# Two graph layers, an expert layer and a dense layer in float32 on one core: a new order and another split of the work in the first layer

## The chip, the cores and the metric

The kernel runs on one core of a Trainium2 chip. The metric is the time of one execution on the device in microseconds (us). TensorE (PE in the profile) multiplies, VectorE (DVE), ScalarE (ACT) and GpSimd (POOL) work on elements, and SyncE (SP) issues most of the DMAs.

## What is computed

The adjacency matrix M is 4096 x 4096, the input x is 4096 x 128, all in float32. Each of two blocks is a graph layer and an expert (FFN) layer. The change touches only the first graph layer of the first block, called the first layer here:

```
A = M / (sum of M over rows + 1e-8)
W = A where A > 1e-6, else 0
T = h @ W_in + b_in
agg = (W^T @ T) / (sum of W over rows + 1e-8)    (T itself for a column without an entry)
out = agg @ W_out + b_out + h @ W_self + b_self
h = relu(layernorm(out) * gamma + beta)
```

h is the layer norm of x. D_in is 128, the hidden width of this layer is 256. A second layer of the same form (256 to 128) follows with the same M, then a gate and eight experts, then in the second block M times the hidden state and a routed FFN.

## The kernel before

M is cut into eight blocks of 512 columns (`NB = 8`, `BW = 512`). A block is 4096 x 512 float32, 8.4 MB, and is loaded in four quarters of 2 MB into one of two slots of `ring` (two slots of 128 KB a partition in all). The first layer goes over the blocks from the last to the first, block k of this order in slot k % 2. Of each block three engines make use while it is in its slot:

- DVE adds its 32 row tiles into two halves of R (`add_quarter`, L826: 15 adds of 128 x 1024 a block) and folds these (`fold`, L834) into pA, 128 partial sums a column. PE sums pA over the partitions with a matrix of ones (`sums`, L1310), and by columns (L1312), into SR and SM.
- ACT checks with an activation that counts (`check`, L533) whether any entry lies in the range in which the threshold could matter. DVE reduces the counts to `bad` (`verdict`), PE sums it (`sum_verdict`, L1323), and DVE reads the flag (L872) and masks the block only if it is set (`mask_if_needed`). With these inputs it is not.
- PE multiplies the block by S, the normalised input (`products`, L1330: 32 products of 128 x 512 a block, each in two records in the trace).

PE forms these column sums twice a block: `raw_sums(k)` (for the threshold) and again at the start of the step (`sums(BT, s_ms)`, the sums after a possible mask). DVE writes the threshold of each block (L853), the indicator of empty columns (L893, 128 x 512), and in `scales` a chain of small operations on 128 x 4 (L894 to L913).

What follows for a block, one step later: DVE adds product and indicator to aT (`collect` and L967). PE multiplies aT and hT (the transposed input, staged by POOL, turned by `turn_h`, copied by ACT at L546) by the joint weights, 256 wide (`out_rows`, L1345 and L1346), tiles 0 and 1 and then 2 and 3. POOL makes the bias rows (L691, L693). DVE adds all three into z1 (`out_tiles`), takes the moments (L785, L788), waits for the inverse root from POOL (L669) and normalises (L937). PE turns z1 (`turn_z`, L1358), ACT applies gamma, beta and relu (L552), PE multiplies by the weights of the second layer (`layer2_products`, L1369), and DVE adds biases into U and R (`layer2_inputs`). POOL adds the node's own T for empty columns (`own_T2`).

Nothing is scheduled by a planner. Each engine has its queue written out by hand in its `step`, and semaphores tie them. On PE the pieces stand between the products: out_rows 0, 1 after product 12 of the step, raw_sums after 18, out_rows 2, 3 after 21, turn_z after 30, sum_verdict after 31, and after the last product layer2_products and turn_h. The first product of a step waits for `s_clean`, which DVE sets once the flag is read and the block masked or not. DVE's order in a step is scales, layer2_inputs, aT, quarter 3 and fold of the next block, out_tiles 0, 1, quarter 0 of the block after it, thresholds, out_tiles 2, 3, normalise, verdict, the flag, quarters 1 and 2. SP issues quarter q of block k+2 once PE is through quarter q of block k, and the last one after the block (`refill`).

Of the kernel before, what the change touches and what calls it, by code (L numbers as in the profile page):

```python
# [69 lines left out]
SUM_MAX = 4.0 / 4096.0 / THRESH  # L70
FMAX = 3.4028234e38
# [6 lines left out]
def build(nc, A, out):  # L78
    ctx = ExitStack()
    with ctx:  # L80
# [37 lines left out]
        sumc, rs_, ws_, rw_, nn = [small[:, 4 * i:4 * i + 4] for i in range(5)]  # L118
        rbp, cc = [[small[:, 72 + 8 * i + 4 * j:76 + 8 * i + 4 * j] for i in range(2)] for j in range(2)]
# [13 lines left out]
        pA, thr, aT, hT, hs = [part(BW * i, BW) for i in range(5)]  # L133
        pre = [part(5 * BW + DH * i, DH) for i in range(2)]
# [93 lines left out]
        zeros = R[:, t_at + 1920:t_at + 1920 + BW]  # L228
# [27 lines left out]
        s_ms = sem("s_ms")  # L256
# [3 lines left out]
        s_thr = sem("s_thr")  # L260
# [9 lines left out]
        s_hs = sem("s_hs")  # L270
# [3 lines left out]
        s_o1u = sem("s_o1u")  # L274
        s_pre = sem("s_pre")
# [82 lines left out]
        def peeled1(eng, step):  # L358


            for k in range(NB):
                step(k, k % 2, k // 2, {d: 0 <= k + d < NB for d in (-2, -1, 1, 2)})

        def scan(eng, k):


            return (NB - 1) - k

# [16 lines left out]
        def _(sp):  # L385
            load_quarter(sp, adjc, scan(sp, 0), 0, 0)
# [3 lines left out]
            for q in range(1, 4):  # L390
                load_quarter(sp, adjc, scan(sp, 0), 0, q)
            for dst, name in WEIGHTS:
                sp.dma_start(dst, A[name]).then_inc(s_wts, 16)
            for q in range(2):
                load_quarter(sp, adjc, scan(sp, 1), 1, q)

            sp.wait_ge(s_thrst, 16)
            for q in range(2, 4):
                load_quarter(sp, adjc, scan(sp, 1), 1, q)

            def store_thr(k):
                sp.wait_ge(s_thr, k + 1)
                alone(sp)
                sp.dma_start(thr_d[ds(scan(sp, k), 1), :], thr[0:1, :]).then_inc(s_thrst, 16)

            def refill(k, slot):
                for q in range(3):

                    sp.wait_ge(s_quart, (k - 2) * 3 + q + 1)
                    alone(sp)  # L410
                    load_quarter(sp, adjc, scan(sp, k), slot, q)
                store_thr(k - 1)
                sp.wait_ge(s_agg, k - 1)
                alone(sp)
                load_quarter(sp, adjc, scan(sp, k), slot, 3)

            refill(2, 0)
# [5 lines left out]
            for q in range(4):  # L423
                n = E1 * CAP // 4
                sp.dma_start(disp_d[q * n:(q + 1) * n, :].rearrange("(p t) r -> p (t r)", p=P), fill).then_inc(s_fill, 16)
            for k in range(3, NB):
                refill(k, k % 2)
# [15 lines left out]
            def tail_inputs():  # L443

                sp.wait_ge(s_u2u, 2 + 2 * NB)
# [76 lines left out]
        def _(act):  # L522
            def check(k, slot, rnd, q):

                if q == 0 and k > 0:
                    act.wait_ge(s_bad, k)
                    alone(act)
                act.wait_ge(s_ring[slot][q], (rnd + 1) * 16)
# [8 lines left out]
            for q in range(4):  # L537
                check(0, 0, 0, q)

            act.wait_ge(s_thr, 1)  # L540
            act.dma_start(thr_d[NB - 1:NB, :], thr[0:1, :]).then_inc(s_thrst, 16)
            act.wait_ge(s_wts, 16 * len(WEIGHTS))

            def evac_hT(k):
                act.wait_ge(s_hTp, k + 2)
                nc.scalar.copy(hT, T[0][:, :]).then_inc(s_hT, 1)  # L546

            def relu_h1(k):

                act.wait_ge(s_zT, k)  # L550
# [5 lines left out]
            def step(k, slot, rnd, has):  # L556
                if has[1]:
                    check(k + 1, 1 - slot, rnd + slot, 2)
                    check(k + 1, 1 - slot, rnd + slot, 3)
                if has[2]:  # L560
                    check(k + 2, slot, rnd + 1, 0)
                    check(k + 2, slot, rnd + 1, 1)
                if has[-1]:
                    relu_h1(k)
                evac_hT(k)

            check(1, 1, 0, 0)
            check(1, 1, 0, 1)
            peeled1(act, step)
            relu_h1(NB)  # L570


# [74 lines left out]
        def _(pool):  # L647
# [31 lines left out]
            def stage(k):  # L679

                pool.wait_ge(s_hTp, k + 1)
                alone(pool)
                nc.gpsimd.tensor_copy(hs, S[:, ds(scan(pool, k) * BW, BW)]).then_inc(s_hs, 1)

            def bias_rows(kk, slot):
                pool.wait_ge(s_msp, kk + 1)
                alone(pool)
                for t in range(BT):
                    pool.wait_ge(s_o1u, kk * BT + t + 1)
                    alone(pool)  # L690
                    nc.gpsimd.tensor_scalar(pre[t % 2], b_io[:, :], cc[slot][:, t:t + 1], None, ALU.mult)  # L691
                    pool.drain()
                    nc.gpsimd.tensor_tensor(pre[t % 2], pre[t % 2], b_all[:, :], ALU.add).then_inc(s_pre, 1)  # L693

            def own_T2(kk):

                blk = scan(pool, kk)
                pool.wait_ge(s_u2u, kk * 2 + 4)
                alone(pool)
                cols = ds(blk * BW, BW)  # L700
# [960 lines left out]
```

## Time and profile before

| | before |
|---|---|
| median of 3 runs | 1170.33 us (1165.82 to 1171.22) |
| the profiled execution | 1171.33 us |
| its span, first to last instruction | 1169.6 us |
| mean granted TensorE clock | 0.965 |
| PE busy | 1049.7 us (90%) |
| DVE busy | 586.1 us (50%) |
| ACT busy | 299.3 us (26%) |
| POOL busy | 303.7 us (26%) |

The profile shows one execution, and its times below count from the first instruction; 1.7 us of the execution lie outside the span. The shares are over the whole kernel; the first layer is roughly its first 390 us, in which DVE is much busier than later. The chain of waits gives DVE's adds (L826) 12% of the whole span, all of it in the first layer. A PE time includes a modelled end of some 0.17 us that overlaps the next instruction.

### The profile page before, as it was taken

How to read it: one execution, taken by the hardware profiler on the slowest of the kernel's cores; microseconds unless marked ns; L12 is line 12 of the kernel's file. 1: busy time of each engine (PE TensorE's matmuls, PEld its weight loads, DVE VectorE, ACT ScalarE, POOL GpSimd, SP SyncE). 2: the span in 40 equal slices, each digit the busy share in tenths (PEclk: the TensorE clock that was granted, in tenths of full speed). 3: DMA queues.
4: the chain of work that ended last, by engine and by line, in shares of the span. 5: the costliest groups of instructions: out<-in, count | busy, mean ns of one | idle time of the engine just before them, and what ended most of it. 6: DMA issues, size and time to landing. Idle time of an engine off the chain costs nothing.

```text
span 1169.6 us, 13701 instructions
## 1 busy us (share of the span) xinstructions
PE 1049.7 (90%) x4004; PEld 610.9 (52%) x4004; DVE 586.1 (50%) x1560; ACT 299.3 (26%) x594; POOL 303.7 (26%) x303
## 2 busy tenths in 40 slices
PE   0598989989999999999996599679999999999996
PEld 0344545545555554444442388424766756667655
DVE  6867778778763323434444168752243332422333
ACT  4542624434400000000000045232212222212222
POOL 4703254354243412222222135541011010110110
PEclk9889999999999999999998699879999999999998
DMA  9859555455400278888671643147354454453200
GB/s 359 331 187 350 208 216 198 166 212 206 154 1 1 80 284 304 312 317 312 266 301 69 248 144 118 50 144 287 145 224 164 181 188 182 179 225 145 82 10 10
DMA packets 44894, 221.00 MB, mean 189 GB/s; under 512 B 6610, under 2 KB 27412, under 8 KB 33170
## 3 DMA queue, kind: packets, MB, share of 16 engines
q1 hardware_dynamic: 41872, 215.47, 49.4%
q0 software_dynamic: 2944, 4.66, 1.2%
q8 instruction: 31, 0.51, 0.2%
q14 instruction: 45, 0.37, 0.1%
q10 hardware_dynamic: 2, 0.00, 0.0%
HBM read 210.68 MB, written 11.62 MB: 190 GB/s over the span
## 4 chain that ended last, share of the span: by engine, by line
PE 67%; DVE 19%; issue 4%; ACT 2%; DVEq 2%; POOL 2%; DMA 1%; SPq 1%; ACTq 0%; POOLq 0%
PE PA L1330 26%; PE PA L1516 19%; DVE R L826 12%; PE O L1555 5%; PE O L1492 3%; PE SR L1555 2%; PE SM L1555 2%; ACT U L595 2%; PE T L1563 1%; PE O L1538 1%; PE PA L1482 1%; PE O L1369 1%; POOL small L669 1%; PE T L1358 1%; PE SR L1421 1%
## 5 line engine op out<-in xcount | busy, mean ns | idle before, releaser
L1516 PE MATMUL PA<-ring,S 128*128 128x512 f32 x512 | 234.5, 603 | 3.7 <-ACT S L613 2.9
L1330 PE MATMUL PA<-ring,S 128*128 128x512 f32 x512 | 232.8, 605 | 0.0
L1330 PE MATMUL PA<-ring,U 128*128 128x512 f32 x512 | 225.6, 595 | 0.0
L826 DVE TENSOR_TENSOR R<-R,ring 128x1024 f32<-128x1024 f32 x112 | 157.3, 1404 | 15.9 <-issue 9.4
L1255 DVE TENSOR_TENSOR U<-ring,work 128x512 f32<-128x512 f32 x128 | 93.7, 733 | 123.8 <-PE SR L1555 49.9
L1330 PEld LDWEIGHTS PA<-ring,S 128*128 128x128 f32 x512 | 96.9, 194 | 105.3 <-issue 104.3
L1330 PEld LDWEIGHTS PA<-ring,U 128*128 128x128 f32 x512 | 95.1, 190 | 106.7 <-issue 106.5
L1516 PEld LDWEIGHTS PA<-ring,S 128*128 128x128 f32 x512 | 94.7, 193 | 106.0 <-issue 100.7
L533 ACT ACTIVATE work<-ring 128x2048 int8<-128x2048 f32 x64 | 122.3, 1910 | 107.0 <-DMA ring<-in_adj_cols 91.6
L774 POOL DMA_DIRECT2D out_x<-work x8 | 6.7, 842 | 285.5 <-DVE work L1281 285.5
L744 POOL DMA_INDIRECT disp_d<-work x32 | 32.2, 1008 | 122.7 <-DVE work L1128 115.4
L1555 PEld LDWEIGHTS O<-work,U 128*128 128x128 f32 x512 | 59.5, 192 | 6.9 <-issue 6.7
L1555 PE MATMUL O<-work,U 128*128 128x64 f32 x512 | 58.9, 274 | 0.0
L756 POOL DMA_INDIRECT y_d<-R,work x40 | 40.9, 1023 | 57.3 <-DVE R L1188 49.7
L638 ACT ACTIVATE U<-O,work 128x64 f32<-128x64 f32 x128 | 33.2, 310 | 71.2 <-PE O L1555 59.4
L1281 DVE TENSOR_TENSOR work<-T,work 128x512 f32<-128x512 f32 x8 | 5.5, 692 | 90.7 <-PE T L1563 90.7
L691 POOL TENSOR_SCALAR work<-b_io,small 128x256 f32<-128x256 f32 x32 | 43.1, 1347 | 21.8 <-DVE work L927 19.2
L666 POOL TENSOR_SCALAR small<-mv 128x4 f32<-128x4 f32 x32 | 7.7, 240 | 149.4 <-DVE mv L788 138.7
L718 POOL TENSOR_TENSOR U<-U,work 128x512 f32<-128x512 f32 x8 | 14.0, 1753 | 109.5 <-ACT work L546 109.5
L581 ACT COPY work<-T 128x512 f32<-128x512 f32 x8 | 4.7, 585 | 137.4 <-PE T L1415 137.4
L552 ACT ACTIVATE work<-T,gb 128x512 f32<-128x512 f32 x16 | 11.6, 773 | 109.2 <-PE T L1358 109.2
L1492 PE MATMUL O<-work,U 128*128 128x128 f32 x320 | 37.9, 278 | 1.0 <-ACT U L595 0.6
(212 smaller groups left out, 1242.1 us busy)
## 6 DMA issues: line engine op xcount, KB each, us to landing
ring<-in_adj_cols SPq DMA_DIRECT2D x56, 2048.0 KB, 7.3
ring<-in_adjT_cols SPq DMA_DIRECT2D x32, 2048.0 KB, 7.2
ring<-in_Wr SPq DMA_DIRECT2D x1, 4096.0 KB, 12.3
ring<-in_Wr SPq DMA_DIRECT2D x2, 2048.0 KB, 13.3
work<-in_w SPq DMA_DIRECT2D x16, 256.0 KB
disp_d<-U SPq DMA_DIRECT2D x4, 650.0 KB, 13.1
work<-disp_d SPq DMA_DIRECT2D x8, 325.0 KB, 3.2
S<-in_x SPq DMA_DIRECT2D x4, 512.0 KB, 8.9
```

The costliest lines, as they stand in the source:

```text
L533: last = nc.scalar.activation(junk, src, ACT.Gelu, scale=GELU_SCALE, accum_out=csum[slot][:, col:col + 1])
L595: nc.scalar.activation(e_hm[:, f * CAP + c * CAP // 2:f * CAP + (c + 1) * CAP // 2], HB[q % 4][:, 0:CAP // 2], ACT.Relu, bias=e_b1[par][:, ...
L638: last = nc.scalar.activation(dst[:, m * BW + s * SEG:m * BW + (s + 1) * SEG], LB[n // SH][:, at:at + SEG], ACT.Relu, bias=b_r[:, ds(e + ( ...
L691: nc.gpsimd.tensor_scalar(pre[t % 2], b_io[:, :], cc[slot][:, t:t + 1], None, ALU.mult)
L744: nc.gpsimd.indirect_dma_start(disp_d, bass.IndirectOffsetOnAxis(ap=idx[:, t:t + 1], axis=0), rows[:, t * ROW:(t + 1) * ROW], None, bounds ...
L756: nc.gpsimd.indirect_dma_start(y_d, bass.IndirectOffsetOnAxis(ap=e_idx[par][:, q:q + 1], axis=0), e_y[par][:, q * D:(q + 1) * D], None, bo ...
L826: nc.vector.tensor_tensor(acc, first if q == 0 and c == 1 else acc, piece, ALU.add)
L1255: nc.vector.tensor_tensor(wst[n % WS], ring[0][l][:, ds(e * (KH * DH), KH * DH)], w_s[:, l * KH * DH:(l + 1) * KH * DH], ALU.add).then_inc ...
L1330: mm = nc.tensor.matmul(out_T[:, :], X[:, t * D:(t + 1) * D], ring[slot][t // HT][:, (t % HT) * BW:(t % HT + 1) * BW], start=n == 0, stop= ...
L1492: mm = nc.tensor.matmul(bank[:, c * D:(c + 1) * D], e_hm[:, f * CAP + q * P:f * CAP + (q + 1) * P], e_w2[par][:, f * D:(f + 1) * D], start ...
L1516: mm = nc.tensor.matmul(PA[slot][:, :], S[:, t * D:(t + 1) * D], ring[1][t // HT][:, (t % HT) * BW:(t % HT + 1) * BW], start=t == 0, stop= ...
L1555: mm = nc.tensor.matmul(LB[g][:, at:at + SEG], wst[n % WS][:, kk * DH + m * P:kk * DH + (m + 1) * P], src[:, kk * BW + s * SEG:kk * BW + ( ...
```

## The change

- The sums are formed once a block on PE (`raw_sums`). Threshold and masked sums are made by DVE only in the branch that masks (`masked_sums`), and the per-node sums are copied to SBUF (`ms`).
- The indicator of empty columns is made by ACT (`empty_cols`, L542) from SR. ACT also writes cc times the bias row into z1 (`bias_rows`, L553), and normalises (L561) with a scale and a bias that POOL makes (`moments`). POOL adds the constant bias in one 128 x 1024 operation (`add_bias`). It stages nothing for `turn_h` any more; PE turns from S. hT is double.
- The order in a step is new on every engine. Block 1's last two quarters no longer wait for a threshold store. The zeros for clearing y_d lie in U rather than R.

The diff, cut to what the orders and these operations are:

```diff
@@ SP
-            for q in range(2):
-                load_quarter(sp, adjc, scan(sp, 1), 1, q)
-            sp.wait_ge(s_thrst, 16)
-            for q in range(2, 4):
-                load_quarter(sp, adjc, scan(sp, 1), 1, q)
+            for q in range(4):
+                load_quarter(sp, adjc, blk(1), 1, q)
...
@@ ACT
+            def empty_cols(k):
...
+                act.wait_ge(s_sums, k + 1)
+                alone(act)
+                nc.scalar.activation(U[:, cols_of(k)], SR[:, :], ACT.Relu, bias=ones[:, 0:1], scale=EMPTY_SCALE).then_inc(s_ind, 1)
...
+            def bias_rows(k):
+                act.wait_ge(s_msp, k + 1)
+                alone(act)
+                for t in range(BT):
+                    last = nc.scalar.activation(z1[:, t * DH:(t + 1) * DH], b_io[:, :], ACT.Copy, scale=cc[k % 2][:, t:t + 1])
+                last.then_inc(s_pre0, 1)
+            def normalise(k):
+                act.wait_ge(s_rstd, k + 1)
+                alone(act)
+                for t in range(BT):
+                    zt = z1[:, t * DH:(t + 1) * DH]
+                    last = nc.scalar.activation(zt, zt, ACT.Identity, bias=nm[:, t:t + 1], scale=rstd[:, t:t + 1])
+                last.then_inc(s_z, 1)
...
+            for k in range(NB):
+                evac_hT(k)
+                if k + 1 < NB:
+                    check(k + 1, 3)
+                if k > 0:
+                    normalise(k - 1)
+                    relu_h1(k - 1)
+                bias_rows(k)
+                if k + 1 < NB:
+                    empty_cols(k + 1)
+                if k + 2 < NB:
+                    for q in range(3):
+                        check(k + 2, q)
...
@@ POOL
+            for k in range(NB):
+                empty_rows(k)
+                if k > 0:
+                    moments(k - 1)
+                add_bias(k)
+                if k > 0:
+                    own_T2(k - 1)
...
@@ DVE
-            def thresholds(k):
...
-                nc.vector.tensor_scalar(thr, SR[:, :], EPS, THRESH, ALU.add, ALU.mult)
...
+            def verdict(k):
+                dve.wait_ge(s_sums, k + 1)
+                alone(dve)
+                nc.vector.tensor_copy(ms, SM[:, 0:BT])
+                nc.vector.tensor_scalar(sumc, SM[:, 0:BT], EPS, None, ALU.add)
+                dve.wait_ge(s_cnt, k + 1)
...
             def scales(k):
-                nc.vector.tensor_scalar(U[:, ds(blk * BW, BW)], SR[:, :], 0.0, None, ALU.is_le)
...
-                dve.wait_ge(s_rstd, k)
-                alone(dve)
-                for t in range(BT):
-                    zt = z1[:, t * DH:(t + 1) * DH]
-                    last = nc.vector.tensor_scalar(zt, zt, mv8[:, t, 0:1], rstd[:, t:t + 1], ALU.subtract, ALU.mult)
...
+            def step(k):
+                if k > 0:
+                    collect(k - 1)
+                if k + 1 < NB:
+                    add_quarter(k + 1, 2)
+                if k > 0:
+                    out_tiles(k - 1)
+                if k + 1 < NB:
+                    add_quarter(k + 1, 3)
+                    fold(k + 1)
+                if k + 2 < NB:
+                    add_quarter(k + 2, 0)
+                if k + 1 < NB:
+                    verdict(k + 1)
+                if k > 0:
                     layer2_inputs(k - 1)
+                if k + 1 < NB:
+                    mask_if_needed(k + 1)
+                    scales(k + 1)
+                if k + 2 < NB:
+                    add_quarter(k + 2, 1)
...
@@ PE
-            def step(k, slot, rnd, has):
                 pe.wait_ge(s_clean, k + 1)
-                sums(BT, s_ms)
-                pe.wait_ge(s_aT, k + 1)
...
+            L1_PIECES = ((2, lambda k: turn_h(k)),
+                         (4, lambda k: k > 0 and out_rows(k - 1, (0, 1))),
+                         (10, lambda k: k > 0 and out_rows(k - 1, (2, 3))),
+                         (18, lambda k: k > 0 and turn_z(k - 1)),
+                         (21, lambda k: k + 1 < NB and raw_sums(k + 1)),
+                         (25, lambda k: k > 0 and layer2_products(k - 1)),
+                         (29, lambda k: k + 1 < NB and sum_verdict(k + 1)))
...
```

How the queues moved, at three places. First PE from the product that sums the verdict (SM) to the next out_rows (O from W_io and W_s), before:

```order
L1323 MATMUL SM<-ones,small 1x1
L1330 MATMUL PA<-ring,S 128x512
L1369 MATMUL O<-W_us,work 128x256 x8
L1351 MATMUL T<-ident,work 128x128 x4
L1310 MATMUL SR<-work,ones 128x512
L1312 MATMUL SM<-ones,work 128x1 x4
L1330 MATMUL PA<-ring,S 128x512 x12
L1345 MATMUL O<-W_io,work 128x256
L1346 MATMUL O<-W_s,work 128x256
```

and now:

```order
L1341 MATMUL SM<-ones,small 1x1
L1348 MATMUL PA<-ring,S 128x512 x5
L1372 MATMUL T<-ident,S 128x128 x4
L1348 MATMUL PA<-ring,S 128x512 x2
L1364 MATMUL O<-W_io,work 128x256
L1365 MATMUL O<-W_s,work 128x256
```

The second sums and layer2_products are gone from this stretch, and 7 products stand in it in place of 13.

Second, DVE around aT (work from PA and U) of the last block, before (the small operations are the end of scales):

```order
L909 TENSOR_TENSOR small<-small 128x4
L911 TENSOR_TENSOR small<-small 128x4
L913 TENSOR_TENSOR small<-small 128x4
L949 TENSOR_TENSOR U<-O,b_us 128x256
L950 TENSOR_TENSOR R<-O,b_us 128x256
L949 TENSOR_TENSOR U<-O,b_us 128x256
L950 TENSOR_TENSOR R<-O,b_us 128x256
L967 TENSOR_TENSOR work<-PA,U 128x512
L826 TENSOR_TENSOR R<-R,ring 128x1024 x4
```

and now:

```order
L951 TENSOR_TENSOR small<-rb,small 128x4
L952 TENSOR_TENSOR small<-small,ne 128x4
L954 TENSOR_TENSOR small<-small,ne 128x4
L848 TENSOR_TENSOR R<-R,ring 128x1024 x4
L989 TENSOR_TENSOR work<-PA,U 128x512
L848 TENSOR_TENSOR R<-R,ring 128x1024 x4
L965 TENSOR_TENSOR work<-O,work 128x256
L967 SCALAR_TENSOR_TENSOR work<-O,small,work 128x256
```

Between scales and aT now stand four adds; layer2_inputs left this place.

Third, DVE from the verdict to the reading of the flag, before:

```order
L788 BN_AGGR mv<-st 128x2 x4
L937 TENSOR_SCALAR work<-work,mv,small 128x256 x4
L862 TENSOR_REDUCE small<-small 128x1
L864 TENSOR_SCALAR small<-small 128x1
L866 SCALAR_TENSOR_TENSOR small<-small 128x1
L872 CAST flags<-SM 1x1
```

and now:

```order
L879 TENSOR_REDUCE small<-small 128x1
L880 TENSOR_SCALAR small<-small 128x1
L882 SCALAR_TENSOR_TENSOR small<-small 128x1
L979 TENSOR_TENSOR U<-O,b_us 128x256
L980 TENSOR_TENSOR R<-O,b_us 128x256
L979 TENSOR_TENSOR U<-O,b_us 128x256
L980 TENSOR_TENSOR R<-O,b_us 128x256
L919 CAST flags<-SM 1x1
```

Between verdict and flag DVE now waits for layer2_products and adds its results.

## Rows read from the trace of the kernel before

**Rows 1.** Busy time by engine in one step (start:end, length, busy us and instructions)
```profile
219.00:263.00 44.00, 40.51 (x134) 22.00 (x134) 34.83 (x62) 18.36 (x21) 18.92 (x14) 1.00 0.50 192
```
**Rows 2.** Timeline of DVE, one step: start, us, instructions, idle before
```profile
226.39 6.17 DVE L826 TENSOR_TENSOR R<-R,ring 128x1024 f32<-128x1024 f32 x4 [0.19 <-issue]
232.75 0.69 DVE L893 TENSOR_SCALAR U<-SR 128x512 f32<-128x512 f32 x1 [0.19 <-issue]
...
235.38 0.16 DVE L913 TENSOR_TENSOR small<-small 128x4 f32<-128x4 f32 x1
...
237.08 0.68 DVE L967 TENSOR_TENSOR work<-PA,U 128x512 f32<-128x512 f32 x1
237.68 7.08 DVE L826 TENSOR_TENSOR R<-R,ring 128x1024 f32<-128x1024 f32 x4
244.94 0.70 DVE L834 TENSOR_TENSOR work<-R 128x512 f32<-128x512 f32 x1 [0.18 <-issue]
245.95 0.42 DVE L925 TENSOR_TENSOR work<-O,work 128x256 f32<-128x256 f32 x1 [0.31 <-issue]
...
255.69 1.41 DVE L785 BATCH_NORM_STATS2 st<-work 128x6 f32<-128x256 f32 x4
257.17 0.38 DVE L788 BATCH_NORM_AGGREGATE mv<-st 128x2 f32<-128x6 f32 x4
259.36 1.38 DVE L937 TENSOR_SCALAR work<-work,mv,small 128x256 f32<-128x256 f32 x4 [1.82 <-POOL small L669]
...
263.08 0.15 DVE L872 CAST flags<-SM 1x1 int32<-1x1 f32 x1 [1.80 <-PE SM L1323]
264.35 5.13 DVE L826 TENSOR_TENSOR R<-R,ring 128x1024 f32<-128x1024 f32 x4 [1.12 <-issue]
```
**Rows 3.** Timeline of PE: pieces of one step, and 18 products of layer two
```profile
220.13 3.62 PE L1369 MATMUL O<-W_us,work 128*128 128x256 f32 x16
...
224.02 1.02 PE L1310 MATMUL SR<-work,ones 128*128 128x512 f32 x2
224.88 0.95 PE L1312 MATMUL SM<-ones,work 128*128 128x1 f32 x8
...
237.86 0.67 PE L1345 MATMUL O<-W_io,work 128*128 128x256 f32 x2 [1.62 <-DVE work L967]
...
260.89 1.06 PE L1358 MATMUL T<-ident,work 128*128 128x128 f32 x8 [1.15 <-DVE work L937]
...
427.93 15.62 PE L1330 MATMUL PA<-ring,U 128*128 128x512 f32 x36
```
**Rows 4.** Groups by line on ACT: busy us, mean ns | idle before
```profile
L552 ACT ACTIVATE work<-T,gb 128x512 f32<-128x512 f32 x16 | 11.6, 773 | 109.2 <-PE T L1358 109.2
L610 ACT ACTIVATE S<-R,work 128x128 f32<-128x128 f32 x24 | 7.4, 387 | 34.2 <-POOL work L669 34.2
```
**Rows 5.** Timeline of POOL beside DVE's adds of 226.39
```profile
224.99 2.34 POOL L718 TENSOR_TENSOR U<-U,work 128x512 f32<-128x512 f32 x1 [9.47 <-ACT work L546]
```
**Rows 6.** Stretches after two stalls of PE; PEclk is third from last
```profile
74.00:80.70 6.70, 6.70 (x15) 3.66 (x14) 4.31 (x9) 4.01 (x4) 0.00 (x0) 0.51 0.19 78
...
108.10:111.40 3.30, 3.30 (x9) 2.65 (x10) 3.15 (x3) 0.00 (x0) 0.00 (x0) 0.52 1.09 367
```
**Rows 7.** Timeline of PE, the first two blocks
```profile
49.51 2.07 PE L1310 MATMUL SR<-work,ones 128*128 128x512 f32 x2 [2.19 <-POOL S L676]
...
73.10 1.52 PE L1310 MATMUL SR<-work,ones 128*128 128x512 f32 x2 [2.64 <-DVE work L834]
...
107.87 1.19 PE L1345 MATMUL O<-W_io,work 128*128 128x256 f32 x2 [4.52 <-issue]
```
**Rows 8.** Timeline of DVE: the last copy before block 0's verdict
```profile
45.05 0.28 DVE L1007 COPY b_us<-O 128x128 f32<-128x128 f32 x1
```
**Rows 9.** Timeline of PE: out_rows of blocks 5 and 7
```profile
324.49 0.67 PE L1345 MATMUL O<-W_io,work 128*128 128x256 f32 x2 [1.19 <-DVE work L967]
...
393.96 0.60 PE L1345 MATMUL O<-W_io,work 128*128 128x256 f32 x2
```

More of the change, by code:

```diff
@@ L118, in build @@
         sumc, rs_, ws_, rw_, nn = [small[:, 4 * i:4 * i + 4] for i in range(5)]
+        ms, nm = [small[:, 64 + 4 * i:68 + 4 * i] for i in range(2)]
         rbp, cc = [[small[:, 72 + 8 * i + 4 * j:76 + 8 * i + 4 * j] for i in range(2)] for j in range(2)]
@@ L130, in part @@
             return work[:, at:at + n]
-        pA, thr, aT, hT, hs = [part(BW * i, BW) for i in range(5)]
-        pre = [part(5 * BW + DH * i, DH) for i in range(2)]
+        pA, thr, aT = [part(BW * i, BW) for i in range(3)]
+        hT = [part(BW * i, BW) for i in (3, 4)]
+        own = part(5 * BW, BW)
         z1 = part(6 * BW, BT * DH)
@@ L953, in collect @@
             def collect(k):
[L955 removed]
+                dve.wait_ge(s_agg, k + 1)
                 alone(dve)
[L957 removed]
+                dve.wait_ge(s_neh, k + 1)
                 alone(dve)
[L960 to L987 removed]
@@ L991, in _ @@
+            add_quarter(0, 0)
+            add_quarter(0, 1)
             dve.wait_ge(s_rstd0, 1)
@@ L1007, in _ @@
             nc.vector.tensor_copy(b_us[:, 0:D], O[1][:, 2 * D:3 * D]).then_inc(s_wready, 1)
-            thresholds(0)
-            verdict(0, 0)
-            mask_if_needed(0, 0)
-            for q in range(3):
-                add_quarter(1, 0, q)
-            peeled1(dve, step)
-            layer2_inputs(NB - 1)
-            collect(NB)
-            nc.vector.tensor_tensor(aT, PA[1][:, :], U[:, 0:BW], ALU.add).then_inc(s_aT, 1)
-            out_tiles(NB, 1, range(BT))
-            normalise(NB)
-            layer2_inputs(NB)
+            verdict(0)
+            mask_if_needed(0)
+            scales(0)
+            for q in range(2):
+                add_quarter(1, q)
+            for k in range(NB):
+                step(k)
+            collect(NB - 1)
+            out_tiles(NB - 1)
+            layer2_inputs(NB - 1)
             dve.wait_ge(s_own, NB)
@@ L1371, in layer2_products, with step @@
                         mm.then_inc(s_u2, 1)
-            def step(k, slot, rnd, has):
-                pe.wait_ge(s_clean, k + 1)
-                sums(BT, s_ms)
-                pe.wait_ge(s_aT, k + 1)
-                products(S, slot, 0, 12, s_quart)
-                if has[-1]:
-                    out_rows(k, (0, 1))
-                products(S, slot, 12, 18, s_quart)
-                if has[1]:
-                    raw_sums(k + 1)
-                products(S, slot, 18, 21, s_quart)
-                if has[-1]:
-                    out_rows(k, (2, 3))
-                products(S, slot, 21, 30, s_quart)
-                if has[-1]:
-                    pe.wait_ge(s_hT, k)
-                    turn_z(k)
-                products(S, slot, 30, 31, s_quart)
-                if has[1]:
-                    sum_verdict(k + 1)
-                products(S, slot, 31, NT, s_quart).then_inc(s_agg, 1)
-                if has[-1]:
-                    layer2_products(k)
-                turn_h(k)
-            raw_sums(0, True)
+            L1_PIECES = ((2, lambda k: turn_h(k)),
[5 more added lines that the diff above has]
+                         (29, lambda k: k + 1 < NB and sum_verdict(k + 1)))
+            def step(k):
+                pe.wait_ge(s_clean, k + 1)
+                if k >= 2:
+                    pe.wait_ge(s_aT, k - 1)
+                done = 0
+                for n, piece in L1_PIECES:
+                    products(S, k % 2, done, n, s_quart)
+                    piece(k)
+                    done = n
+                products(S, k % 2, done, NT, s_quart).then_inc(s_agg, 1)
+            raw_sums(0)
             sum_verdict(0)
             pe.wait_ge(s_hn, 2)
-            peeled1(pe, step)
+            for k in range(NB):
+                step(k)
             def tail_a(k):
```

355 lines of the change are left out of this document (165 added, 190 removed).

## The prediction

> **What bounds the kernel now.** I read the page first: the change touches only the first layer, so only its 390 us count. Next I took busy times by stage. In one step of the first layer PE is busy 40.5 us of 44 and DVE 34.8 [rows 1]. PE looks like the bound, but the timelines say otherwise. PE waits for DVE at three places of each step: 1.62 us before out_rows, until aT is there; 1.15 us before turn_z, until z is normalised [rows 3]; and 0.7 us before raw_sums. DVE waits only 1.82 us for POOL's inverse root, 1.80 us for the flag and 1.12 us in the branch behind it [rows 2]. So **DVE's queue is the chain**: its work, small gaps and three short waits fill the step. From out_rows of block 0 at 107.87 to that of block 5 at 324.49 are five steps [rows 7, 9]: 216.6 us, or **43.3 a step**.
>
> I call the start of the first out_rows in a step s. The question is what s to s will be, when the first s comes, and how long it is from the last full step to out_rows of block 7, which starts layer two at 393.96 [rows 9].
>
> **What goes and what comes, per step.**
> - PE: the second sums go, 1.65 us (1.02 and 0.95 without their modelled ends) [rows 3].
> - DVE: L893 goes to ACT, 0.61 without the end that the next operation overlaps; the threshold, of the same form, 0.61; the normalise 1.3, with its wait of 1.82; a copy, a compare and one drained step of scales, some 0.25. The copy `ms` adds 0.1. About 2.8 us of work and 1.8 of waiting [rows 2].
> - POOL: the staging copy and eight bias operations go, one of 128 x 1024 and two tiny ones come. POOL slows DVE: four adds take 5.13 us when it rests, 6.17 with 2.5 us of it beside them, 7.08 under a long run [rows 2, 5]. Aside from the place named below, I cost its new work at nothing: it lies where DVE has slack.
> - ACT: the indicator 0.7, four bias rows and four normalises of 128 x 256. By 128 x 128 at 0.31 (7.4 us for 24) and 128 x 512 at about 0.7 a time [rows 4], four take 1.6 to 1.9. ACT is busy 18 of 44 us [rows 1] and has room. Only the normalise is on a path.
>
> If nothing else bound, PE's own work would: 32 products 27.5, out_rows 3.5, layer2_products 3.45, turn_z, turn_h, sums and flag 3.1 [rows 3], about 37.5 us a step. I don't believe this, because of the order.
>
> **The loop that remains.** With times from s:
> - PE from s to the flag: four tiles of out_rows 3.5, 25 products at 0.86 (15.62 for 18) 21.5, turn_z 0.87, sums 1.65, layer2_products 3.45, the flag 0.15 [rows 3]: 31.1.
> - Does turn_z wait? PE is there at s+15.55. DVE has two tiles of out_tiles done at s+7.1 (0.9 each), but tile 3 leaves PE only at s+8.7, so the moments end at s+11.6 [rows 2]. Inverse root 1.8, two more small POOL operations 0.5, normalise on ACT 1.75, semaphores: s+15.8. A wait of 0.3. The fold is done at s+18.1, PE wants it at s+19.1: no wait. Sum s+31.4.
> - DVE meanwhile is through with its adds and verdict at s+23.4 and then waits for layer2_products (s+26 and s+27.8) and again for the flag. Here its saved work ends as **idle time**.
> - Then DVE in series: semaphore 0.1, flag to next operation 1.27, scales 2.8 - 0.61 - 0.25 = 1.95, gap 0.2, quarter 1 of the next block but one, gap 0.25, aT 0.68, semaphore 0.1 [rows 2]. The four adds take 5.13 to 7.08; POOL multiplies the indicator by hT just then (2.34 us when contended [rows 5]), which is the case of 6.17. I take 6.1. Sum 10.6.
>
> So s to s is 31.4 + 10.6 = **42.0 us**, 41.0 with uncontended adds, 43.0 with the slowest. PE in the meantime has only 7 products and turn_h, 6.45 us, to do. It then stands still for about 4.15 us, at one place rather than three.
>
> **The clock.** Such a stall has a price in this trace. After 4.52 us of idling at 107.87 the granted clock was 0.52, the level of 1.2 GHz, for 3.3 us; after 2.64 us, followed by one-column products, 0.51 for 6.7 us [rows 6, 7]. The stalls of 1.6 us did nothing. A 3.4 us stretch at half clock costs 1.7. A stall of 4.15 lies between, nearer to the one of 4.52, but when it begins to count probably varies, and part of the slow stretch can fall into the stall itself. I take 1.0 a step between ends of 0 and 1.7. **Forecast per step: 43.0**, ends 41.0 and 44.7.
>
> The Trainium skill (TensorE: Matmul & The Clock Gate, HAM oscillation) says that a kernel whose matmuls pause too long in every iteration starts each one cold. By that rule the full 1.7 would come each step, 43.7, and the steady steps would lose a little; it speaks against this change, and the row at 107.87 agrees with it.
>
> **The start.** Block 0's second sums go, so products begin at 49.5 [rows 7], where POOL's normalised x arrives. DVE's last copy ends at 45.3 [rows 8]; verdict 0.95, flag 0.4, branch 1.3 to 1.5, scales 1.95: 50.2. Fifteen adds of block 1 at 1.3 with gaps 20.5, contention 1, fold 0.9: 72.5. PE needs 18.5 for 21 products and turn_h, plus 2 to 3 for the low clock it has there before too, and so waits briefly. Sums 1.65, eight products 6.9, so the flag goes at 81.1; flag, branch and scales 3.5, adds 6.1, gaps and aT 1.2: **first s at 92**, against 107.87. Why so much: PE does not wait through fold and sums of block 1, and out_rows moves from product 12 of a step to 4. The second part is handed back at the end.
>
> **The end.** The last full step starts five steps later: 92 + 215 = 307. In it there is no quarter 1 to add, so aT is there before PE wants it: 31.4 + 2.6 + 3.4 + 0.43 = 37.9 to the next s. From there 32.1 us of PE work without the sums and 3.4 of products to out_rows of block 7: 35.5. 307 + 37.9 + 35.5 = **380.4, against 393.96: 13.6 us less**. Behind it nothing moves: PE was dense there, z comes 1.1 later from ACT but the bias rows earlier, which is what DVE waited for.
>
> 1171.33 - 13.6 is 1157.7 for the profiled execution; the median of the runs shown is 1.0 below it, so **1157 us**.
>
> **The rivals.**
> 1. *The clock holds.* Same loop, but the stalls cost nothing: 42.0 a step, 5 us less than forecast: 1152. For: the stalls of 1.6 us are harmless. Against: 4.52 was not.
> 2. *Full overlap.* DVE's 12% in the chain of waits is really shed and PE's 37.5 to 38.5 us binds. 5 x 4.5 less than forecast: 1134. This needs DVE to pass flag, scales, adds and aT in the 6.5 us PE has for it; the rows give 10.6.
> 3. *The clock halves in every step, or ACT's share is longer.* 43.7 to 45.4 a step (slow stretches of 3.4 or 6.7 us): 1161 to 1169. At the upper end no change.
> 4. *Slower.* The mechanism: a slow stretch in each step makes PE late at sum_verdict and, if it begins again at the wait before turn_z, a second one follows. Two stretches of 6.7 us cost 6.7 a step: 48.7, 1157 + 28 = 1185. It decides from 46.6 a step, where the gain of start and end is used up and 6 us more. For: the row of 2.64 us with 6.7 us of low clock. Against: there one-column products followed; here wide ones do.
>
> The change does what it says, by the orders of the queues; the branch is not taken before nor after.
>
> **How the numbers follow.** Forecast 0.45, clock holds 0.20, full overlap 0.06, every step slow 0.21, slower 0.08. A measurement here can tell about 0.5%, 6 us, from no change. Faster by over 6 us: the first three, and half of the fourth, with a little off for a first s that comes late (a stall of 3 us before raw_sums would add a slow stretch): 0.76. Same 0.16, slower 0.08. The unknown costs (adds 41.0 to 43.0 a step, clock 0 to 1.7, first s 90 to 94, runs that differ by 5 us) make 1145 to 1168, which leaves out full overlap and slower.
>
> **What the profile after would show.** s at 92, and 42 to 43.7 us a step; PE's one long stall of about 4 us before out_rows, released by DVE's aT; DVE idle before layer2_inputs and the flag; PEclk under 1.00 in stretches behind some stalls; out_rows of block 7 at 380. I am wrong if the stall before out_rows is under 2 us, if turn_z waits over 1 us (ACT's normalise then sets the loop), or if layer two and later differ by more than 3 us.

## The result, and the profile after

The changed kernel takes **1190.2 us** (1188.9 to 1191.4, four runs) against 1170.35: a ratio of 1.0177 with an interval of 1.0148 to 1.0207. It is slower by 1.8%, where 1.1% faster was forecast, and lies outside the range. Times differ between chips: on one of those used below the kernel before took 1178.9 us. So kernels are compared by their ratio to the kernel before, run in the same group.

PE's timeline of one step after the change (start, us, what, idle before and its releaser), from one out_rows to the next:

```profile
239.41 1.19 PE L1364 MATMUL O<-W_io,work 128*128 128x256 f32 x2 [3.81 <-issue]
240.40 1.06 PE L1365 MATMUL O<-W_s,work 128*128 128x256 f32 x2
...
242.75 5.31 PE L1348 MATMUL PA<-ring,S 128*128 128x512 f32 x12
...
249.62 7.03 PE L1348 MATMUL PA<-ring,S 128*128 128x512 f32 x16
258.93 1.39 PE L1380 MATMUL T<-ident,work 128*128 128x128 f32 x8 [2.28 <-ACT work L561]
260.12 4.17 PE L1348 MATMUL PA<-ring,S 128*128 128x512 f32 x6
264.13 1.02 PE L1334 MATMUL SR<-work,ones 128*128 128x512 f32 x2
...
276.29 0.19 PE L1341 MATMUL SM<-ones,small 128*1 128x1 f32 x2
...
287.17 1.19 PE L1364 MATMUL O<-W_io,work 128*128 128x256 f32 x2 [4.05 <-issue]
```

A step is 47.8 us here, and 47.7 in the mean of five, from 96.23 to 334.91. Before it was 43.3 [rows 7, 9]. Each step has two stalls of PE, 3.8 to 4.05 us before out_rows, as forecast, and 2.3 to 2.7 before turn_z, which was not. Behind each the first instructions are slow: the first half of out_rows (four tile products) takes 3.3 us in place of 1.7, three products behind turn_z 4.0 in place of 2.6. Windows of time show why (start:end, length, busy us and counts, granted clock third from last):

```profile
239.50:242.60 3.10, 3.10 (x8) 2.47 (x9) 2.95 (x3) 2.27 (x3) 0.00 (x0) 0.51 0.00 0
242.70:256.60 13.90, 13.90 (x37) 6.67 (x36) 10.36 (x21) 1.64 (x2) 3.29 (x4) 1.00 0.48 170
259.70:262.90 3.20, 3.20 (x7) 1.64 (x7) 2.96 (x3) 2.54 (x6) 0.00 (x0) 0.50 0.55 236
```

PE runs at half clock, 1.2 GHz, behind both stalls, in every step; between them the clock is 1.00. The stretches after a stall in the kernel before read the same [rows 6].

DVE in the same step, from the moments to the flag and on to aT:

```profile
252.51 0.38 DVE L813 BATCH_NORM_AGGREGATE mv<-st 128x2 f32<-128x6 f32 x4
252.81 5.09 DVE L848 TENSOR_TENSOR R<-R,ring 128x1024 f32<-128x1024 f32 x4
...
266.08 0.16 DVE L873 COPY small<-SM 128x4 f32<-128x4 f32 x1 [3.27 <-PE SM L1336]
...
271.35 0.42 DVE L979 TENSOR_TENSOR U<-O,b_us 128x256 f32<-128x256 f32 x1 [4.38 <-PE O L1391]
...
276.63 0.15 DVE L919 CAST flags<-SM 1x1 int32<-1x1 f32 x1 [2.80 <-PE SM L1341]
278.16 0.18 DVE L938 RECIPROCAL small<-small 128x4 f32<-128x4 f32 x1 [1.39 <-issue]
...
280.05 6.03 DVE L848 TENSOR_TENSOR R<-R,ring 128x1024 f32<-128x1024 f32 x4
286.38 0.69 DVE L989 TENSOR_TENSOR work<-PA,U 128x512 f32<-128x512 f32 x1 [0.30 <-issue]
```

DVE idles for 3.27 us before the sums, 4.38 before layer2_inputs and 2.80 before the flag. The work taken from it, 2.8 us a step, became waiting. Its own chain from flag to aT lasts 10.5 us, in which PE has 7 products and turn_h.

Over the first layer: the first out_rows comes at 96.2 (before 107.9), that of block 7 at 414.5 (before 394.0 [rows 9]), so the layer is 20.5 us later at the point where layer two starts. The median is 19.9 longer; after that point the profiled execution wins back 2.7 us, which no run here explains.

### The profile page after: what moved, and what is told of

The parts are those of the page before. It is cut to its first block, busy times and chain, and to the rows that moved or that the text cites. A ratio compares the mean times of both kernels' runs of the same rounds, so it can differ in the third digit from the quotient of the medians.

```text
span 1187.4 us, 13419 instructions
## 1 busy us (share of the span) xinstructions
PE 1048.8 (88%) x3924; PEld 609.0 (51%) x3924; DVE 551.8 (46%) x1500; ACT 333.9 (28%) x666; POOL 245.6 (21%) x255
## 4 chain that ended last, share of the span: by engine, by line
PE 76%; DVE 8%; issue 4%; ACT 4%; POOL 2%; DMA 1%; DVEq 1%; SPq 1%; POOLq 1%; ACTq 0%
PE PA L1348 32%; PE PA L1532 18%; PE O L1571 5%; DVE R L848 3%; PE O L1508 3%; ACT U L620 2%; PE SR L1571 2%; PE SM L1571 2%; PE O L1391 2%; PE O L1364 2%; ACT work L561 1%; PE T L1579 1%; PE O L1365 1%; PE O L1554 1%; PE T L1380 1%
## 5 line engine op out<-in xcount | busy, mean ns | idle before, releaser
L1348 PE MATMUL PA<-ring,S 128*128 128x512 f32 x512 | 242.7, 623 | 3.0 <-POOL S L701 3.0
L1532 PE MATMUL PA<-ring,S 128*128 128x512 f32 x512 | 231.5, 596 | 4.7 <-ACT S L638 3.7
L1348 PEld LDWEIGHTS PA<-ring,S 128*128 128x128 f32 x512 | 100.8, 202 | 110.3 <-issue 105.6
L848 DVE TENSOR_TENSOR R<-R,ring 128x1024 f32<-128x1024 f32 x112 | 145.1, 1295 | 7.5 <-issue 0.9
L1532 PEld LDWEIGHTS PA<-ring,S 128*128 128x128 f32 x512 | 93.2, 190 | 105.3 <-issue 98.4
L1571 PEld LDWEIGHTS O<-work,U 128*128 128x128 f32 x512 | 59.4, 192 | 6.9 <-issue 6.7
L561 ACT ACTIVATE work<-work,small 128x256 f32<-128x256 f32 x32 | 16.6, 590 | 122.8 <-POOL small L729 122.8
L1364 PE MATMUL O<-W_io,work 128*128 128x256 f32 x64 | 25.4, 487 | 22.8 <-issue 22.8
L1508 PEld LDWEIGHTS O<-work,U 128*128 128x128 f32 x320 | 36.3, 192 | 3.2 <-ACT U L620 3.2
```

What stands on the lines that cost most here:

```text
L561: last = nc.scalar.activation(zt, zt, ACT.Identity, bias=nm[:, t:t + 1], scale=rstd[:, t:t + 1])
L848: nc.vector.tensor_tensor(acc, first if q == 0 and c == 1 else acc, piece, ALU.add)
L1348: mm = nc.tensor.matmul(out_T[:, :], X[:, t * D:(t + 1) * D], ring[slot][t // HT][:, (t % HT) * BW:(t % HT + 1) * BW], start=n == 0, stop= ...
L1364: nc.tensor.matmul(O[t % 2][:, 0:DH], aT[:, t * P:(t + 1) * P], W_io[:, :], start=True, stop=True)
L1508: mm = nc.tensor.matmul(bank[:, c * D:(c + 1) * D], e_hm[:, f * CAP + q * P:f * CAP + (q + 1) * P], e_w2[par][:, f * D:(f + 1) * D], start ...
L1532: mm = nc.tensor.matmul(PA[slot][:, :], S[:, t * D:(t + 1) * D], ring[1][t // HT][:, (t % HT) * BW:(t % HT + 1) * BW], start=t == 0, stop= ...
```

## The experiments

Theory A: the loop is the one of the prediction (PE from out_rows to the flag, then DVE from the flag to aT); its length exceeds 42.0 us because z is late, since POOL's small operations now run beside DVE's adds, and because the clock falls behind both stalls. The rivals: ACT's longer chain is the loop; POOL is slow for another reason; the clock falls for another cause; DVE's or the loads' own time binds.

Steps are means from the out_rows of block 0 to that of block 5. "Stalls" are PE's in a middle step, before out_rows / turn_z / raw_sums. PEclk is the granted clock from 100 to 380 us.

| kernel | ratio (95%) | step, us | stalls, us | PEclk |
|---|---|---|---|---|
| before | 1 | 43.3 | 1.6 / 1.15 / 0.7 | 0.99 |
| changed | 1.0177 (1.0148 to 1.0207) | 47.7 | 3.8 / 2.3 / 0 | 0.93 |
| e0, changed again | 1.0181 (1.0147 to 1.0214) | 47.5 | 3.8 / 2.3 / 0 | 0.93 |
| e1, turn_z later | 0.9979 (0.9954 to 1.0004) | 43.0 | 3.65 / 0 / 0 | 0.96 |
| e2, adds held | 1.0065 (1.0044 to 1.0085) | 45.5 | 4.0 / 0.5 / 0.4 | 0.96 |
| e3, warm | 1.0048 (1.0032 to 1.0065) | 44.8 | 0.4 / 2.3 / 0 | 0.99 |
| e5, e1 and e3 | 0.9886 (0.9854 to 0.9919) | 41.8 | 0.2 / 0 / 0 | 1.00 |
| e6, DVE's order | 1.0091 (1.0056 to 1.0125) | 46.4 | 0 / 2.3 / 3.6 | 0.94 |
| e7, PE's order | 0.9835 (0.9804 to 0.9865) | 41.3 | 2.0 / 0.6 / 0 | 1.00 |
| e4, both orders | 0.9690 (0.9668 to 0.9712) | 38.8 | 0 / 0.6 / 0 | 1.00 |
| e8, e4, normalise on DVE | 1.0011 (0.9997 to 1.0026) | 45.2 | 0 / 0 / 3.6 | 0.92 |
| e9, changed, sums twice | 0.9993 (0.9980 to 1.0007) | 44.5 | 1.0 / 2.3 / 0 | 0.98 |
| e11, e4, sums twice | 0.9772 (0.9756 to 0.9789) | 40.6 | 0 / 0.6 / 0 | 1.00 |
| e10, e4, one product later | 0.9618 (0.9602 to 0.9634) | 38.0 | 0 / 0 / 0 | 1.00 |

### The yardstick

The changed kernel, unedited.

> The changed kernel itself, unedited, as the yardstick of this group, since the kernel before took 1178.9 us on the chip of the last group rather than 1170.3. All theories: 1.015 to 1.02 of the kernel before, steps of 47.7 us.

1188.6 us, 1.0181, steps of 47.5: it repeats.

### turn_z behind raw_sums

```diff
-                         (18, lambda k: k > 0 and turn_z(k - 1)),
-                         (21, lambda k: k + 1 < NB and raw_sums(k + 1)),
+                         (21, lambda k: (k + 1 < NB and raw_sums(k + 1), k > 0 and turn_z(k - 1))),
```

> The changed kernel, but PE turns z behind raw_sums (both after product 21) rather than after product 18. In the changed kernel PE waits 2.3 to 2.7 us before turn_z in six steps, and the low clock behind that stall costs another 1.6 to 1.75. Theory A (the late z and the low clock behind it are what made a step 47.7 us rather than 42.0): both go, a step becomes 43.7 us, six steps give 24 us, so about 1166 us. Rival B (the loop hangs on ScalarE's chain of normalise, relu and bias rows, and the stall only moves to layer2_products or the flag): the step stays over 46.5 us and the time within 5 us of 1190.

Measured 1175.2 us beside 1178.9 of the kernel before, 0.9979. Against the ratio of the changed kernel this is 2.0% less, some 23 us. The stall before turn_z is gone and the steps are 41.9, 43.3, 41.9, 43.7 and 44.3 us: 43.0 in the mean. The two of 41.9 us are those without a slow stretch. One of them begins with a stall of 3.65 us before out_rows, behind which the clock stays at 1.00. The ten runs lie between 1170.3 and 1182.0 us, the longer ones at a lower mean clock (0.952 against 0.963 at the ends). Theory A holds, rival B falls.

### DVE's adds held back

```diff
                     out_tiles(k - 1)
+                    dve.wait_ge(s_rstd, k)
+                    alone(dve)
                 if k + 1 < NB:
                     add_quarter(k + 1, 3)
```

> The changed kernel, but DVE waits for the inverse root before it adds quarter 3, so nothing of DVE runs beside POOL's four small operations. In the changed kernel these take 3.7 us beside DVE's adds, in the kernel before the two of them took 1.5 with DVE idle. Theory A (contention makes z late): the four take 2.0 to 2.3 us, turn_z waits under 1 us, and no slow stretch follows: 44 to 45 us a step, about 1170 us; DVE's lost 2.3 us fall into its idle time. Rival C (the small operations of POOL are slow for another reason, such as more of them in a row): they stay near 3.7 us, the fold comes 4 us later, and the time is equal or worse, 1190 to 1210 us.

POOL's four operations in the changed kernel:

```profile
253.09 1.01 POOL L723 TENSOR_SCALAR small<-mv 128x4 f32<-128x4 f32 x1 [17.14 <-DVE mv L813]
254.18 1.18 POOL L724 TENSOR_SCALAR small<-mv 128x4 f32<-128x4 f32 x1
255.32 1.02 POOL L727 TENSOR_TENSOR small<-small,neg_half 128x4 f32<-128x4 f32 x1
256.48 0.20 POOL L729 TENSOR_TENSOR small<-small 128x4 f32<-128x4 f32 x1
```

and with the adds held back:

```profile
246.10 0.23 POOL L723 TENSOR_SCALAR small<-mv 128x4 f32<-128x4 f32 x1 [17.07 <-DVE mv L813]
246.41 0.19 POOL L724 TENSOR_SCALAR small<-mv 128x4 f32<-128x4 f32 x1
246.56 1.03 POOL L727 TENSOR_TENSOR small<-small,neg_half 128x4 f32<-128x4 f32 x1
247.73 0.20 POOL L729 TENSOR_TENSOR small<-small 128x4 f32<-128x4 f32 x1
```

From first start to last end they take 3.59 against 1.83 us, the way from the end of the moments to turn_z shrinks from 6.0 to 4.3 us, and the stall before turn_z falls from 2.3 to 0.5. So the first two operations, 0.2 us long by themselves, wait out a DVE add each, and rival C falls. The Trainium skill (SBUF — State Buffer, Who interferes with whom) has this: a DVE instruction with two SBUF inputs contends with a GpSimd instruction that reads SBUF, and whoever comes second waits until the other's instruction is over. This trace agrees: the delays of 0.8 and 1.0 us are under the 1.27 us of an add. The four adds run from 252.81 to 257.90, so by estimate one ends at 254.1 and the next at 255.4, and the two operations end at 254.10 and 255.36. The third and fourth operation are not lengthened; the third starts at 255.32, near the end of an add.

The step, 45.5, was a little above the 44 to 45 expected, and the gain 13 us rather than 20: raw_sums now waits 0.4 us, and two slow stretches behind out_rows last 6.8 us, not 3.4.

### Four products to fill the stall

```diff
-                         (4, lambda k: k > 0 and out_rows(k - 1, (0, 1))),
+                         (4, lambda k: k > 0 and (keep_warm(4 if k < NB - 1 else 0, S[:, 0:BW], T[1]), out_rows(k - 1, (0, 1)))),
```

> The changed kernel with four products of 128x512 into an unused bank of PSUM (their result is not read) ahead of out_rows 0 and 1 in the steps with a stall of 3.8 to 4.0 us there; they take 3.4 us at full clock. Theory A (the clock falls because PE stands still): PEclk stays 1.00 behind this stall, out_rows takes 1.7 us rather than 3.3, five or six steps give 1.6 us each, so 8 to 10 us less: about 1181 us. If the shorter step also keeps the second slow stretch, nothing more. Rival D (the clock at out_rows falls for another cause than the stall): the time stays 1190 us.

Ratio 1.0048, so some 15 us less than changed, more than the 8 to 10 expected. Four of the five steps are 44.3 to 44.5 us. The clock no longer falls at out_rows, and behind the stall of 2.3 us before turn_z, which is still there, it falls in one step of six only, the one in which this stall is 2.66 us and not 2.28. So the stall at out_rows causes its slow stretch (rival D falls). The second, for a stall of 2.3 us, depends on more than its length, since in the changed kernel it came each time.

### Both single edits

> The changed kernel with both single edits: PE turns z behind raw_sums, and four products of 128x512 whose result is not read fill the stall before out_rows. Theory A: with neither a late z nor any low clock the loop is what the walk in the prediction gave without a clock term, 42.0 us a step plus 0.5 because the four products start a moment late or end behind aT: 42.0 to 42.5, PEclk 1.00 from 100 to 400 us, and 28 to 32 us less than the changed kernel in the same group. Rival F (the low clock comes from the load on the chip and wanders whatever PE does): slow stretches remain and the steps stay at 43 to 44 us as with the first edit alone.

It combines the two diffs above.

```profile
100.00:380.00 280.00, 277.84 (x857) 149.03 (x856) 173.65 (x343) 126.30 (x166) 66.00 (x55) 1.00 0.43 167
```

PEclk is 1.00 throughout, steps are 41.9, 41.6, 41.8, 42.0 and 41.9 us, and the time is 1155.5 us, 33 less than e0, a little more than the 28 to 32 expected. This is the loop of the prediction, 42.0 without a clock term. Rival F falls. POOL's operations are as slow here as in the changed kernel; the 1.8 us that they lose fit in before turn_z at its new place.

### DVE's half of a better order

```diff
                 if k + 1 < NB:
-                    add_quarter(k + 1, 2)
+                    add_quarter(k + 1, 1)
                 if k > 0:
                     out_tiles(k - 1)
                 if k + 1 < NB:
+                    add_quarter(k + 1, 2)
                     add_quarter(k + 1, 3)
...
                     scales(k + 1)
-                if k + 2 < NB:
-                    add_quarter(k + 2, 1)
```

> Only DVE's half of the new order: aT straight behind scales, quarter 1 and out_tiles, then quarters 2 and 3. PE's queue as in the changed kernel. Theory A: aT comes early, but the fold now comes at s+23.4 while PE has raw_sums at s+19 to 21, so PE waits 2 to 4 us there, and z is 2.3 us late: 42 to 43 us a step without slow stretches, up to 45 with them; 15 to 30 us less than the changed kernel. Rival G (the adds between the flag and aT are the whole matter): 39 us a step or less.

Steps of 42.4 to 48.5 us, 46.4 in the mean, where at most 45 was expected; ratio 1.0091, 9 us less than e0 and not 15 to 30. The loop between flag and aT is gone; raw_sums takes its place, with PE coming too early for the fold:

```profile
246.51 1.09 PE L1378 MATMUL T<-ident,work 128*128 128x128 f32 x8 [2.29 <-ACT work L561]
247.44 2.74 PE L1346 MATMUL PA<-ring,S 128*128 128x512 f32 x6
253.79 2.07 PE L1332 MATMUL SR<-work,ones 128*128 128x512 f32 x2 [3.62 <-DVE work L856]
255.66 1.71 PE L1334 MATMUL SM<-ones,work 128*128 128x1 f32 x8
257.23 6.42 PE L1346 MATMUL PA<-ring,S 128*128 128x512 f32 x8
```

In this step the low clock lasts 10.2 us, from 252.4 on: the sums and four products take 9.7 us, and 5.3 in the step at full clock. In the other steps it lasts 3.4 or 6.8 us. Rival G falls: the adds alone are not the matter.

### PE's half

```diff
-                         (18, lambda k: k > 0 and turn_z(k - 1)),
-                         (21, lambda k: k + 1 < NB and raw_sums(k + 1)),
-                         (25, lambda k: k > 0 and layer2_products(k - 1)),
-                         (29, lambda k: k + 1 < NB and sum_verdict(k + 1)))
+                         (20, lambda k: k > 0 and turn_z(k - 1)),
+                         (23, lambda k: k > 0 and layer2_products(k - 1)),
+                         (24, lambda k: k + 1 < NB and raw_sums(k + 1)),
+                         (27, lambda k: k + 1 < NB and sum_verdict(k + 1)))
```

> Only PE's half of the new order: turn_z after product 20, layer2_products after 23, raw_sums after 24, the verdict's sum after 27. DVE's queue as in the changed kernel, so four adds still stand between flag and aT. Theory A: z is in time, the flag goes at about s+29.4, DVE's 10.7 us follow: 40 to 42 us a step, with a stall of 2.5 to 4 us before out_rows that sometimes costs a slow stretch; 30 to 40 us less than the changed kernel. Rival H (DVE's idle time is filled and its queue binds): 43 us or more.

Steps of 41.2 to 41.6 us, ratio 0.9835, some 40 us less than the changed kernel. The stall before out_rows is 2.0 to 2.4 us, less than the 2.5 to 4 expected, and the clock never falls behind it. DVE's idle time is used and its queue does not bind (rival H falls).

### Both halves

> The changed kernel in another order: DVE collects aT straight behind scales and adds quarter 1 after it, with quarter 2 behind out_tiles; PE has turn_z after product 20, layer2_products after 23, raw_sums after 24 and the verdict's sum after 27. Theory A (the adds between the flag and aT, and the place of turn_z, are all that keeps PE's work of 37.5 us a step from being the bound): no stall over 1 us, no slow stretch, 38 to 39 us a step, six steps give over 50 us: 1130 to 1140 us. Rival E (DVE's queue, then about 35 us a step with no idle left, or the later loads bind): 41 to 43 us a step, 1155 to 1165 us.

38.8 us a step, ratio 0.9690, which at 1170 us would be 1134. Rival E falls: with aT early and turn_z near its z, PE's work is the bound.

### All four pieces one product later

The places in e4 become 21, 24, 25 and 28.

> The reordered kernel with turn_z, layer2_products, raw_sums and the verdict's sum each one product later (21, 24, 25, 28). Theory A (PE is the bound, its one stall is the 0.57 us before turn_z): 38.1 us a step, ratio 0.965 to 0.968. Rival K (DVE comes next at once): 38.7 us or more, since flag, scales and aT move later by 0.86 us.

1125.9 us, **0.9618: by the ratios 45 us less than the kernel before, 65 less than the changed one**. A middle step of it on PE, without a stall, and DVE's aT 1.2 us before PE wants it:

```profile
199.40 1.88 PE L1346 MATMUL PA<-ring,S 128*128 128x512 f32 x4
201.12 0.59 PE L1362 MATMUL O<-W_io,work 128*128 128x256 f32 x2
...
219.16 1.04 PE L1378 MATMUL T<-ident,work 128*128 128x128 f32 x8
...
231.50 0.19 PE L1339 MATMUL SM<-ones,small 128*1 128x1 f32 x2
...
239.03 0.59 PE L1362 MATMUL O<-W_io,work 128*128 128x256 f32 x2
```

```profile
199.26 0.69 DVE L989 TENSOR_TENSOR work<-PA,U 128x512 f32<-128x512 f32 x1
```

Rival K falls. The gain was more than the 0.57 us a step: block 1's raw_sums no longer waits either (2.2 us in e4, with a slow stretch behind it), so out_rows of block 0 comes at 86.8 and not 90.1.

### The second sums, in the changed kernel and in e4

The sums of the kernel before, put back at the start of each step on data already there, with a result that is not read:

```diff
                 pe.wait_ge(s_clean, k + 1)
                 if k >= 2:
                     pe.wait_ge(s_aT, k - 1)
+                    pe.wait_ge(s_h1T, k - 1)
+                nc.tensor.matmul(T[1][:, :], ones[:, :], S[:, 0:BW], start=True, stop=True)
+                for t in range(BT):
+                    nc.tensor.matmul(T[1][:, t:t + 1], S[:, t * P:(t + 1) * P], ones[:, 0:1], start=True, stop=True)
```

> The changed kernel with a second group of column-sum products at the start of every step, as the kernel before has them (into an unused bank, on data already there, the result not read), 1.65 us of PE a step. Theory A (in the changed kernel's loop PE stands still there, so dropping the second sums bought nothing): the stall before out_rows shrinks by 1.65 us, the steps do not grow, and may shrink by 1.6 where the shorter stall no longer lowers the clock: ratio 1.005 to 1.018 of the kernel before. Rival J (PE's work counts): steps of 49.4 us, ratio 1.026 to 1.03.

Ratio 0.9993 against 1.0177: **1.65 us of needless work a step makes the changed kernel 1.8% faster**. The stall before out_rows is 1.0 to 1.4 us, the clock stays up there, and steps alternate between 43.4 (clock 1.00) and 45.3 us (one slow stretch behind turn_z):

```profile
226.53 0.67 PE L1364 MATMUL O<-W_io,work 128*128 128x256 f32 x2 [0.99 <-issue]
...
244.52 1.09 PE L1380 MATMUL T<-ident,work 128*128 128x128 f32 x8 [2.28 <-ACT work L561]
```

The ratio is below the band expected, 1.005 to 1.018. Of the gain 2 to 3.5 us come ahead of the steps: the first out_rows is at 92.7, against 96.2 in the changed kernel and 94.6 in e0. The rest fits the clock: three slow stretches from there on in place of twelve. Rival J falls.

> The reordered kernel with the same second group of sums at the start of each step. Theory A (PE is the bound there, so each us of PE counts): 40.3 us a step, eight steps give 13 us, ratio 0.979 to 0.981. Rival L (it still hides behind something): under 39 us a step, ratio 0.969.

Steps of 40.6 us, 1.8 more than e4, ratio 0.9772, just under the 0.979 to 0.981 expected. Where PE is the bound the same work costs its full price a step. Rival L falls.

### The normalise back on DVE, in e4

```diff
                 stats(lambda t: z1[:, t * DH:(t + 1) * DH], BT).then_inc(s_mv, 1)
+                dve.wait_ge(s_rstd, k + 1)
+                alone(dve)
+                for t in range(BT):
+                    zt = z1[:, t * DH:(t + 1) * DH]
+                    last = nc.vector.tensor_scalar(zt, zt, mv8[:, t, 0:1], rstd[:, t:t + 1], ALU.subtract, ALU.mult)
+                last.then_inc(s_z, 1)
```

and ACT's `normalise` is not called.

> The reordered kernel of this study (38.7 us a step) with the normalise back on DVE behind the moments, DVE waiting for POOL's inverse root. It gives DVE 1.3 us of work and about 1.8 of waiting a step; DVE has aT ready 1.7 us before PE wants it. Theory A (once the order is right, the split counts, because DVE is nearly full): the step grows by up to 1.4 us to 39.5 to 40.2, so 5 to 10 us slower than the reordered kernel, ratio 0.974 to 0.978 of the kernel before. Rival I (DVE still has slack, the split buys nothing): 38.2 to 38.8 us a step, since z is then earlier, ratio 0.968.

Ratio 1.0011, steps of 45.2 us. The sign was right, the size was not. I had priced 3.1 us against the slack before aT, but the fold stands between and has none:

```profile
206.09 2.08 PE L1336 MATMUL SR<-work,ones 128*128 128x512 f32 x2 [3.67 <-DVE work L854]
207.96 1.71 PE L1338 MATMUL SM<-ones,work 128*128 128x1 f32 x8
```

PE waits 3.6 us for it, 3.0 more than e4 waits anywhere in a step, and then runs at half clock for 6.8 us (10.2 in this step), which costs 3.4: together the 6.4 us a step. So the normalise on ACT, one part of the change's split, is worth 3.2% in this order. This includes DVE's wait for the inverse root and the low clock; no run puts the normalise at another place of DVE's queue.

## Why the prediction was wrong

- **What bounds the kernel, and the loop that remains: right.** PE's long stall before out_rows was forecast at 4.15 us and is 3.8 to 4.0. DVE's idle time before layer2_inputs and the flag is where it was said. Flag to aT was put at 10.6 us and is 10.5. With z in time and the clock up, e5 measures 41.8 a step where the walk said 42.0.
- **"I cost its new work at nothing", said of POOL, and "Inverse root 1.8, two more small POOL operations 0.5": this step failed.** The 1.8 were read from rows in which DVE waited idle for POOL [rows 2]. The change takes this wait away and lets DVE add in the meantime. I had priced POOL's contention against DVE's adds and not the adds' against POOL. POOL's four operations take 3.59 us beside the adds and 1.83 without (e2). From the end of the moments to turn_z it takes 6.0 us, not 4.2; with the adds held back it is 4.3. PE waits 2.3 before turn_z, not 0.3: **2.0 us a step**. A wait of over 1 us there was named as a sign of being wrong, but with ACT's normalise as its cause; this takes 2.1 us where 1.75 was forecast, and the rest is POOL's.
- **The clock, "I take 1.0 a step": this step failed.** The slow stretch at out_rows costs 1.6 in every step. The one at turn_z, which I did not have, costs 1.7: from turn_z to the sums it takes 5.2 us, and 3.5 in e3. e3 has 44.4 us in each of the four steps in which the clock stays up, with z as late as in the changed kernel: the clock is **3.3 us a step**. 42.0 + 2.0 + 3.3 is 47.3; the 0.4 that are missing to 47.7 stay open.
- The first s came at 96.2, not 92: the fold of block 1 was 1.5 us later and the stall before raw_sums, 3.2 us, brought slow products. The prediction named this stall but let it take only chance away.
- From the out_rows of block 5 to that of block 7 took 79.6 us, not 73.4, since this stretch holds one more turn_z with its stall and slow stretch, and the part of a step after out_rows with the slow clock.
- The sum of the misses, of the first s, of five steps and of the end: 4.2 + 5 x 4.7 + 6.2 = 34 us, from 380.4 to 414.5 for the last out_rows.
- **The rival that won** was the slower one, in its mechanism: a slow stretch at out_rows and a second one at the wait before turn_z. It was given 8%. It argued for 6.7 us a step by stretches of 6.7 us each; what came was 1.6, 1.7 and a late z. Its argument against, that wide products follow, did not keep the slow stretches from beginning, in any step, and in e1 and e2 not from lasting 6.8 us either. I also kept the two stalls independent, though the row of 2.64 us [rows 7] had already shown a clock falling behind a stall of that size.
- The Trainium skill (TensorE: Matmul & The Clock Gate, HAM oscillation) describes a kernel that starts cold, at half clock, in every iteration. It deserved more weight than I gave it: the changed kernel has a granted clock of 0.50 to 0.51 behind both stalls of each step.

## What to carry to other kernels

A wait that you remove may have been the quiet in which another engine was fast: price the contention both ways, above all for short operations beside long two-input adds. Here several short stalls were cheaper than the same time in one, so look at how long PE's longest stall becomes and not only at their sum. Work that leaves a busy engine pays only once the order lets the next bound take it up: here the change as a whole cost 1.8%, while in the better order (e4 against e8) the normalise part of its split gains 3.2%. No run has the new order with the old split throughout, or the new split in the old order, so how the 1.8% divide between the two is not shown.

## What the runs showed of the hardware

- Adding 1.65 us of unused products to each step made the changed kernel 1.8% faster (e9), mostly since stalls of 1.0 to 1.4 us before out_rows leave the clock up (six of six). Stalls of 3.8 to 4.05 us there were followed by half clock each time: in 18 of 18, in the changed kernel, e0, e1 and e2.
- In between it is not settled by length. Of the stalls before out_rows those of 2.0 to 2.4 us in e7 never lowered the clock (five). Four of 3.1 us ahead of the first out_rows lowered it twice (changed, e2) and twice not (e0, e1), and two of 3.65 us in e1 lowered it once.
- Before turn_z the stalls of 2.6 to 2.7 us lowered it in all five cases (one each in changed, e0, e3, e6 and e9). Those of 2.3 us did in the changed kernel and e0 in every step, in e9 in two of five, and in e3 and e6 in none. What decides there was not tried.
- A slow stretch lasted 3.4 us in each step of the changed kernel. It lasted 6.8 us twice each in e1, e2 and e6 and five times in e8, and 10.2 us once each in e6 and e8. In e6 and e8 the one-column products of the sums were among the first work behind the stall, as at 73.10 in the kernel before [rows 7]; in e1 and e2 only wide products followed, so narrow ones are not needed for a long stretch.
